# Attention A of a hybrid block on one core: output sums kept in PSUM over runs of head pairs, the norms inside the slots, sine products from PSUM

## The chip, the cores and the metric

The kernel runs on one core of a Trainium2 chip. The metric is the device time of one execution in microseconds (us). The times below are of three executions, and one more execution was profiled: all durations come from that one.

## The reference, cut to what matters

The program is a chain of four residual blocks over `x` of shape (8, 256, 256): attention A, a layer of experts, attention B, the experts again, each on a layer norm of `x`. The change touches attention A alone:

```
x = x + attn_a(layernorm(x));  x = x + ffn(layernorm(x));  x = x + attn_b(layernorm(x));  x = x + ffn(layernorm(x))

attn_a(x):                                # 16 heads, 2048 tokens, width 256
  q = x @ q_a_w.T @ q_b_w.T               # per head 64 plain + 64 rotated
  ckv = x @ kv_a_w.T                      # 64 compressed + 64 shared rotated keys
  k_pass, v = split(ckv[:, :64] @ kv_b_w.T)
  q_rot, k_rot = rope(q_rot), rope(k_rot) # (x0 cos - x1 sin, x1 cos + x0 sin)
  p = softmax([q_pass, q_rot] @ [k_pass, k_rot].T)   # 256 keys for each of 8 sequences
  return (p @ v, heads joined) @ o_w.T
```

## The kernel before, in words

Attention A is `attention_a` (from line 515). The 2048 tokens are four groups of 512 (`NG` = 4, `G` = 512), each of two sequences; the 16 heads are eight pairs (`HP` = 8). The work is 32 **slots**: slot n takes head pair n // 4 over token group n % 4, so one pair of heads goes over all four groups before the next begins. A slot has four **pairs** j = 0 to 3 (two sequences times two heads), and a pair is one 128x512 bank of scores.

Products that must be exact to fp32 are made of three fp32r matmuls (`matmul3`, lines 120 to 122) on upper and lower parts that ACT (upper, a cast) and DVE or POOL (lower, a subtraction) split.

The order of the work is written out by hand: each engine has a `step(n, j)` that lists what it does in that step, and all engines run the steps in the same order, tied by semaphores alone. In step (n, j):

- PE: the scores of the pair that lies six ahead (`LEAD` = 6) into bank `S(j)`, of which there are two; at j = 0 and 1 the query projection of slot n+3 for head h = j (`project_a`, five matmuls of 512 columns, lines 502 to 506) into `PROJ(h)`; at j = 2 the mix of probabilities and values of slot n (`mix`, line 668); the output product of a slot in two halves (`output`), the first at j = 3 of slot n+1, the second at j = 0 of slot n+2. The scores of pair g wait for the exponentials of pair g-2, which read the same bank.
- DVE: the row maxima of that pair (`row_max`, L846), the 32x32 transposes of the probabilities of the pair before it (`turn_squares`, L853), at j = 0 the product of the mixed values with the inverse sums (`normalise`, L869), at j = 0 and 1 the cosine product of the projection (`rope`, L481 through `times_table`), at j = 2 one sine product (`sines`), at j = 1 and 2 the addition of half an output bank to `x` (`add_out`, L874), at j = 3 the inverse of the row sums (`invert`, L858 and L861).
- ACT: the exponentials (`exps`, L771, two per pair), the upper part of the mixed values (`mixed_hi`), at j = 0 and 1 the swap of the two halves of the rotated rows out of PSUM (`swap_a`, L469 and L470, two copies of 32x512), at j = 2 and 3 the upper parts of the queries (`queries_hi`, L761).
- POOL: the lower part of the mixed values (L976), for head 0 the sine product (L481), for both heads the sum of cosine and sine products (`rotate`, L963), the lower parts of the queries (L971).
- SP, the queue that issues all DMAs: four DMAs that move the turned squares of each half slot (`move_squares`, L586), four that store the inverse sums (`store_inverse`, L592), two that load them spread over the partitions (`load_inverse`, L599), and once per head pair the weights (`load`, L579).

A rotated query is thus made so: PE projects, DVE multiplies all 128 rows with the cosines into `raw`, ACT copies rows 96 to 127 and 64 to 95 of the same PSUM bank, swapped, into `swapped`, POOL or DVE multiplies these with the sines in place, POOL adds.

The weights of a head pair are **folded** before use: matmuls on the staged weights (`fold_product`, L428, and `fold_output_product`, L511), upper parts on ACT (L440, L749), lower parts on DVE (L825, L830) and POOL (L982). The fold of the query weights of pair it lies in slot 4(it-2)+3, that of the output weights in the second slot of pair it-1; both keep two sets, taken in turn (`it % 2`).

Each half of an output product is closed in its slot (`start=True, stop=True`) and added to `x` two slots later: 64 additions of 128x512. In the last slots the layer norm of the next block begins: `norm_stats` (lines 59 to 67), `norm_rstd` on POOL (L73), `norm_rows` (L81), transposes on PE (L92), `norm_hi` (L100) and `norm_lo` (L108), groups 0 to 2 within or behind slots 30 and 31, all eight transposes of a group in a row into the two `PROJ` banks; group 3 is finished by the experts' block, whose first products (L1632) start at its opening.

## Time and profile before

| | |
|---|---|
| device time, median of 3 runs | 1533.96 us (1531.46 to 1535.32) |
| device time of the profiled execution | 1535.29 us |
| span of the profiled execution | 1533.5 us |
| mean granted clock of TensorE | 0.987 |
| PE busy | 1463.5 us, 95% |
| DVE busy | 1171.0 us, 76% |
| ACT busy | 835.8 us, 55% |
| POOL busy | 612.6 us, 40% |
| attention A's slots, first to last `aa_mixed` | 79.8 to 386.2 us |

How to read it: the device time is the span and about 1.8 us around it. A busy PE is not PE at its peak, since the ends of matmuls are modelled and overlap with the next one; how fast a stretch of matmuls goes is read from their starts. The busy shares are means over four blocks with different limits, and the change concerns only the stretch from about 54 us (the opening's end) to about 397 us (the first product of the experts).

### The profile page before, as it was taken

The numbers are of one execution on the slowest core, as the hardware profiler recorded it, in microseconds if no ns is written. First come the engines' busy times: TensorE is split into PE (matmuls) and PEld (weight loads), VectorE is DVE, ScalarE is ACT, GpSimd is POOL, SyncE is SP. The second block draws the span as 40 slices with busy tenths as digits, with TensorE's granted clock in tenths as the row PEclk, the third lists the DMA queues.
The fourth block names the chain that finished last, engine by engine and source line by source line (L and its number), as shares of the span: only waits on it lengthen the run. The fifth ranks groups of instructions, "written<-read, shape, count | busy, mean of one in ns | idle before, by whom it ended". The sixth has DMA issues, their size and how long they took to land. (4 is left out here: it accounts for less than half of the span.)

```text
span 1533.5 us, 26670 instructions
## 1 busy us (share of the span) xinstructions
PE 1463.5 (95%) x8904; PEld 1262.6 (82%) x8904; DVE 1171.0 (76%) x2661; ACT 835.8 (55%) x2040; POOL 612.6 (40%) x484
## 2 busy tenths in 40 slices
PE   8899999998799999988999999999999879999998
PEld 6677777776688888877899999989999868888887
DVE  7889999999765555587888888888888777555554
ACT  4788888885432333326766666666666433333322
POOL 2577777875100000017766666666666210000000
PEclk9899999999999999998999999999999999999999
DMA  2265555555210000003222222213222200010001
GB/s 101 53 161 142 154 145 151 148 129 149 82 41 22 22 21 0 1 1 91 62 70 61 71 63 64 75 42 80 73 50 49 56 22 21 21 42 21 0 0 56
DMA packets 73155, 100.16 MB, mean 65 GB/s; under 512 B 10304, under 2 KB 63552, under 8 KB 73024
## 3 DMA queue, kind: packets, MB, share of 16 engines
q1 hardware_dynamic: 73024, 98.55, 24.3%
q8 instruction: 66, 1.08, 0.3%
q14 instruction: 65, 0.53, 0.1%
HBM read 37.56 MB, written 2.23 MB: 26 GB/s over the span
## 5 line engine op out<-in xcount | busy, mean ns | idle before, releaser
L1834 DVE TENSOR_TENSOR f_hidden<-ps,f_silu 128x512 f32<-128x512 f32 x128 | 87.6, 689 | 201.7 <-PE ps L122 201.6
L481 POOL TENSOR_TENSOR ab_swapped<-ab_swapped,const 128x512 f32<-128x512 f32 x126 | 162.9, 1293 | 167.6 <-ACT ab_swapped L476 167.6
L1725 ACT ACTIVATE f_silu<-ps 128x512 f32<-128x512 f32 x128 | 76.3, 598 | 276.8 <-PE ps L122 276.8
L120 PE MATMUL ps<-xh,f_wl 128*128 128x512 f32 x512 | 203.2, 397 | 1.6 <-DVE f_hidden L1834 1.6
L121 PE MATMUL ps<-xl,f_wh 128*128 128x512 f32 x512 | 202.8, 396 | 0.0
L122 PE MATMUL ps<-xh,f_wh 128*128 128x512 f32 x512 | 202.5, 396 | 0.0
L1536 POOL TENSOR_TENSOR ab_qk<-ab_qk,ab_swapped 128x512 f32<-128x512 f32 x126 | 172.5, 1369 | 9.9
L1304 ACT ACTIVATE ab_probs<-ab_probs,ab_negmax 128x128 f32<-128x128 f32 (+1 forms) x256 | 114.6, 448 | 82.6 <-DVE ab_negmax L1407 80.6
L73 POOL TENSOR_TENSOR rstd<-shifted,minus_half 128x4 f32<-128x4 f32 x16 | 16.2, 1013 | 339.6 <-DVE shifted L67 339.6
L771 ACT ACTIVATE aa_probs<-ps,aa_negmax 128x256 f32<-128x256 f32 x256 | 119.2, 471 | 47.1 <-DVE aa_negmax L846 44.0
L120 PE MATMUL ps<-f_wh,f_hl 128*128 128x256 f32 x512 | 144.2, 282 | 0.4 <-DVE x L1850 0.4
L121 PE MATMUL ps<-f_wl,f_hh 128*128 128x256 f32 x512 | 143.9, 281 | 0.0
L122 PE MATMUL ps<-f_wh,f_hh 128*128 128x256 f32 x512 | 143.8, 281 | 0.0
L1431 DVE SCALAR_TENSOR_TENSOR x<-ps,ab_inv,x 128x256 f32<-128x256 f32 x256 | 118.8, 465 | 7.8 <-PE ps L122 3.1
L1733 ACT CAST f_hh<-f_hidden 128x512 fp32r<-128x512 f32 x128 | 78.8, 617 | 77.4 <-DVE f_hidden L1834 77.4
L481 DVE TENSOR_TENSOR ab_qk<-ps,const 128x512 f32<-128x512 f32 x128 | 87.2, 687 | 41.2 <-PE ps L122 40.8
L122 PEld LDWEIGHTS ps<-xh,f_wh 128*128 128x128 f32 x512 | 96.3, 188 | 23.4
L120 PEld LDWEIGHTS ps<-xh,f_wl 128*128 128x128 f32 x512 | 96.4, 188 | 23.1 <-DVE f_hidden L1834 2.4
L121 PEld LDWEIGHTS ps<-xl,f_wh 128*128 128x128 f32 x512 | 96.4, 188 | 20.4
L120 PE MATMUL ps<-xh,b_wl 128*128 128x512 f32 x256 | 105.9, 414 | 4.3 <-ACT ab_swapped L476 3.5
L1417 DVE STREAM_TRANSPOSE ab_squares<-ab_probs 128x384 f32<-128x384 f32 x128 | 109.7, 858 | 0.0
L1850 DVE SCALAR_TENSOR_TENSOR x<-ps,f_col,x 128x256 f32<-128x256 f32 x256 | 107.5, 476 | 1.6 <-PE ps L122 1.5
(210 smaller groups left out, 4377.5 us busy)
## 6 DMA issues: line engine op xcount, KB each, us to landing
ab_probsT<-ab_squares SPq DMA_DIRECT2D x128, 192.0 KB, 3.6
aa_probsT<-f_stages SPq DMA_DIRECT2D x128, 128.0 KB, 2.6
b_stages<-keys SPq DMA_DIRECT2D x128, 128.0 KB, 2.7
f_stages<-wf_in SPq DMA_DIRECT2D x16, 768.0 KB, 4.5
aa_spread<-aa_inv_line SPq DMA_DIRECT2D x64, 128.0 KB, 3.0
b_stages<-wb_qkv_in SPq DMA_DIRECT2D x8, 768.0 KB, 6.3
a_stage<-wa_in SPq DMA_DIRECT2D x8, 608.0 KB, 4.3
x<-x_in SPq DMA_DIRECT2D x4, 512.0 KB, 7.0
```

Of the source, the lines that this page charges most:

```text
L120: nc.tensor.matmul(out, ll, rh, start=start, stop=False)
L121: nc.tensor.matmul(out, lh, rl, start=False, stop=False)
L122: return nc.tensor.matmul(out, lh, rh, start=False, stop=stop)
L481: return engine.tensor_tensor(by_batch(out), by_batch(src), table(c, rows, col), ALU.mult)
L771: ins = nc.scalar.activation(probs[:, j, q, :], S(j)[:, q * T:(q + 1) * T], ACT.Exp, bias=negmax[:, j, q:q + 1], accum_out=total[:, s % 2, ...
L1304: ins = nc.scalar.activation(probs[:, j, span[q]], probs[:, j, span[q]], ACT.Exp, scale=-1.0, bias=negmax[:, j, q:q + 1], accum_out=total[ ...
L1417: nc.vector.transpose(out=squares[:, s % 2, :, :, j, :], in_=probs[:, j].rearrange("p (k i b) -> p b k i", k=3, b=4)).then_inc(squares_don ...
L1431: nc.vector.scalar_tensor_tensor(out=c.x[:, at, :], in0=bank[:, h * D:(h + 1) * D], scalar=inv[:, s, 2 * h + t // 2, t % 2:t % 2 + 1], in1 ...
L1536: nc.gpsimd.tensor_tensor(rows, rows, other, ALU.add).then_inc(rotated, 1)
L1733: nc.scalar.copy(hh[:, s % 2, m, :], hidden[:, m, :]).then_inc(hi_done, 1)
L1834: nc.vector.tensor_tensor(hidden[:, m, :], UP(m), silu[:, m, :], ALU.mult).then_inc(hid_done, 1)
L1850: ins = nc.vector.scalar_tensor_tensor(out=c.x[:, at, :], in0=OUT(i)[:, t, :], scalar=col[:, e, at:at + 1], in1=c.x[:, at, :], op0=ALU.mul ...
```

## The change

1. **Order of the slots.** `RUN_HEADS = [(0,), (1, 2, 3), (4, 5, 6, 7)]`: run 0 is pair 0 over the four groups (slots 0 to 3), run 1 takes for each group the pairs 1, 2, 3 in turn (slots 4 to 15), run 2 the pairs 4 to 7 (slots 16 to 31).
2. **Output in PSUM.** Within a run the output products of one group add up in the same bank: `start` only where a slot opens a run for its group, `stop` and `add_out` only where it closes one. 24 additions are left of 64.
3. **Folds.** Query and output weights are folded together in one piece (`fold`): PE at j = 3 of slots 0, 1, 5, 10, 12, 14, ACT and DVE at j = 0 of the next slot, POOL's part in the next slot too; the loads are issued by SP at the end of slots 0, 1, 2, 6, 11, 13 (its own order), each behind a wait for POOL's part of the fold before. Four sets of query weights and a set of output weights for each pair live partly in corners of `xh` and `xl` that nothing else needs then.
4. **Sines.** DVE multiplies rows 64 to 127 of the PSUM bank with the sines straight behind the cosine product, into rows 0 to 63 of `swapped`; only then is `rope_read` raised, for which ACT's swap waits. The swap copies rows 32 to 63 and 0 to 31 of `swapped` (SBUF) to rows 64 to 127; POOL's sum is now a difference. POOL's and DVE's sine products on `swapped` go.
5. **Norms in the slots.** Group g of the next block's norm for g = 0, 1, 2 goes to slots 21, 25, 29 and the two behind each: statistics at j = 2, `norm_rstd` at the end of POOL's slot, rows at j = 0 of the next, four transposes into the bank `FOLDED` at j = 2 and four at j = 0 of the slot after, each split on ACT and DVE at j = 3 and j = 1.
6. **The end.** The last slot's output goes into the same `OUT` banks; 12 filling matmuls stand before and 12 behind it.

The diff, cut to its core:

```diff
+    RUN_HEADS = [(0,), (1, 2, 3), (4, 5, 6, 7)]
+        RUNS = [(it, s) for its in RUN_HEADS for s in range(NG) for it in its]
+        RUN_OF = [run * NG + s for run in range(len(RUN_HEADS)) for s in range(NG) for _ in RUN_HEADS[run]]
+        opens = lambda n: n == 0 or RUN_OF[n] != RUN_OF[n - 1]
+        closes = lambda n: n == SLOTS - 1 or RUN_OF[n] != RUN_OF[n + 1]
+        FOLD_SLOT = {2: 0, 3: 1, 4: 5, 5: 10, 6: 12, 7: 14}
+        LOAD_SLOT = {2: 0, 3: 1, 4: 2, 5: 6, 6: 11, 7: 13}
+        FINISH = {4 * g + 2 * HP + 5: g for g in range(NG - 1)}
...
         def _(sp):
-                if s == 2 and it + 2 < HP:
-                    load(it + 2)
+                if n in loads:
+                    load(loads[n])
...
         def _(pe):
+            def fold(it):
+                pe.wait_ge(stage_in, 16 * (it + 1))
+                pe.wait_ge(wo_lo, it)
+                fold_product(nc, FOLD(it)[:, 0:P], stage, 0).then_inc(fold_ready, 1)
+                pe.wait_ge(fold_ready, it)
+                fold_product(nc, FOLD(it)[:, P:2 * P], stage, 1)
+                fold_output_product(nc, FOLD(it)[:, 2 * P:], stage).then_inc(wo_ready, 1)
...
             def output(n, i):
+                if opens(n):
+                    after(pe, out_added, 2 * RUN_OF[n] + i - 1)
-                    ins = matmul3(nc, bank[:, t * D:(t + 1) * D], ..., True, True)
+                    ins = matmul3(nc, OUT(i)[:, t * D:(t + 1) * D], ..., opens(n) and t == 0, closes(n) and t == 1)
...
             def step(n, j):
+                if j == 3 and n in folds:
+                    fold(folds[n])
                 if j == 2:
                     mix(n, 0)
                     mix(n, 1)
+                if j == 2 and finish(n - 1) is not None:
+                    turn_rows(finish(n - 1), 0)
+                if j == 0 and finish(n - 2) is not None:
+                    turn_rows(finish(n - 2), 1)
...
         def _(act):
             def swap(n, h):
                 act.wait_ge(rope_read, 2 * n + h + 1)
                 after(act, rotated, 0 if n == 1 else 2 * n + h - 1)
-                swap_a(nc, first_bank(n, h), swapped_of(n, h)).then_inc(swap_done, 1)
+                turned = swapped_of(n, h)
+                nc.scalar.copy(turned[64:96], turned[32:64])
+                nc.scalar.copy(turned[96:128], turned[0:32]).then_inc(swap_done, 1)
...
         def _(dve):
             def rope(n, h):
-                times_table(nc.vector, c, raw_of(n, h), first_bank(n, h), ALL_ROWS, C_COSA).then_inc(rope_read, 1)
+                times_table(nc.vector, c, raw_of(n, h), first_bank(n, h), ALL_ROWS, C_COSA)
+                after(dve, swap_done, 0 if n == 1 else h + 1 if n == 2 else m - 1)
+                times_table(nc.vector, c, swapped_of(n, h)[0:64], first_bank(n, h)[64:128], ROT_ROWS, C_SINA).then_inc(rope_read, 1)
...
             def step(n, j):
+                if j == 0 and n - 1 in folds:
+                    fold(folds[n - 1])
-                if j == 2 and n + 3 < SLOTS:
-                    sines(n + 3, 1)
-                if j in (1, 2) and n >= 2:
+                if j in (1, 2) and n >= 2 and closes(n - 2):
                     add_out(n - 2, j - 1)
+                if j == 2 and finish(n) is not None:
+                    normalise_stats(finish(n))
+                if j == 0 and finish(n - 1) is not None:
+                    norm_rows(nc, c, norm, dve, finish(n - 1))
+                if j == 3 and finish(n - 1) is not None:
+                    norm_lower(finish(n - 1), 0)
+                if j == 1 and finish(n - 2) is not None:
+                    norm_lower(finish(n - 2), 1)
...
         def _(pool):
             def rotate(n, h):
-                if n < 3:
-                    pool.wait_ge(sin_done, 2 * n + h + 1)
-                elif h == 1:
-                    pool.wait_ge(sin_done, n + 4)
-                else:
-                    pool.wait_ge(swap_done, 2 * n + h + 1)
-                    times_table(nc.gpsimd, c, other, other, ROT_ROWS, C_SINA).then_inc(side_done, 1)
-                    pool.wait_ge(side_done, n - 2)
+                pool.wait_ge(swap_done, 2 * n + h + 1)
                 pool.wait_ge(rope_read, 2 * n + h + 1)
-                nc.gpsimd.tensor_tensor(rows, rows, other, ALU.add).then_inc(rotated, 1)
+                nc.gpsimd.tensor_tensor(rows, rows, other, ALU.subtract).then_inc(rotated, 1)
...
+                if n - 1 in folds:
+                    fold_rest_parts(folds[n - 1])
```

## Rows read from the trace of the kernel before

**Rows 1.** Waits in 40 to 400 us: us in total, times, longest.

```profile
ACT aa_probs L771 <- DVE aa_negmax L846: 44.0, 36, 1.8
...
PEld ps L120 <- ACT aa_probs L771: 24.1, 45, 0.9
...
DVE a_wl L825 <- ACT a_wh L440: 8.3, 6, 1.4
...
DVE a_wol L830 <- ACT a_woh L749: 7.1, 7, 1.5
```

**Rows 2.** DVE's timeline over one slot: start us, us, engine, line.

```profile
190.31 0.65 DVE L846 TENSOR_REDUCE aa_negmax<-ps 128x2 f32<-128x512 f32 x1
...
191.50 0.65 DVE L869 TENSOR_TENSOR aa_mixed<-ps,aa_spread 128x512 f32<-128x512 f32 x1
192.08 0.67 DVE L481 TENSOR_TENSOR a_raw<-ps,const 128x512 f32<-128x512 f32 x1
192.68 0.67 DVE L846 TENSOR_REDUCE aa_negmax<-ps 128x2 f32<-128x512 f32 x1
...
193.89 0.65 DVE L481 TENSOR_TENSOR a_raw<-ps,const 128x512 f32<-128x512 f32 x1
...
195.66 0.69 DVE L853 STREAM_TRANSPOSE keys<-aa_probs 128x512 f32<-128x512 f32 x1
196.38 1.44 DVE L481 TENSOR_TENSOR a_swapped<-a_swapped,const 64x512 f32<-64x512 f32 x1
197.85 0.69 DVE L874 TENSOR_TENSOR x<-ps,x 128x512 f32<-128x512 f32 x1
198.46 0.68 DVE L846 TENSOR_REDUCE aa_negmax<-ps 128x2 f32<-128x512 f32 x1
...
201.27 0.65 DVE L869 TENSOR_TENSOR aa_mixed<-ps,aa_spread 128x512 f32<-128x512 f32 x1
```

**Rows 3.** Groups by line and form, whole span: busy us, mean ns, idle before.

```profile
L469 ACT COPY a_swapped<-ps 32x512 f32<-32x512 f32 x62 | 35.8, 578 | 1.6 <-DVE a_raw L481 0.2
...
L481 DVE TENSOR_TENSOR a_swapped<-a_swapped,const 64x512 f32<-64x512 f32 x33 | 31.4, 952 | 1.5 <-ACT a_swapped L470 0.5
```

**Rows 4.** Timelines of ACT, PE, DVE at the hand-overs of scores.

```profile
175.92 0.47 ACT L771 ACTIVATE aa_probs<-ps,aa_negmax 128x256 f32<-128x256 f32 x1
...
176.99 0.39 PE L120 MATMUL ps<-kh,a_ql 128*128 128x256 f32 x1 [0.51 <-ACT aa_probs L771]
...
364.89 0.39 PE L120 MATMUL ps<-kh,a_ql 128*128 128x256 f32 x1
...
365.89 0.69 DVE L846 TENSOR_REDUCE aa_negmax<-ps 128x2 f32<-128x512 f32 x1 [0.19 <-PE ps L122]
```

**Rows 5.** PE's timeline over slots with and without a fold.

```profile
177.80 0.40 PE L502 MATMUL ps<-q1h,a_wl 128*128 128x512 f32 x1
...
181.65 1.37 PE L428 MATMUL ps<-a_stage 64*128 64x64 f32 x8
...
187.98 0.40 PE L502 MATMUL ps<-q1h,a_wl 128*128 128x512 f32 x1
...
202.32 0.65 PE L511 MATMUL ps<-a_stage 128*64 128x256 f32 x4
```

**Rows 6.** DVE's timeline: mixed values of slots 0 and 29.

```profile
79.82 0.69 DVE L869 TENSOR_TENSOR aa_mixed<-ps,aa_spread 128x512 f32<-128x512 f32 x1 [0.24 <-DMA aa_spread<-aa_inv_line]
...
369.06 0.69 DVE L869 TENSOR_TENSOR aa_mixed<-ps,aa_spread 128x512 f32<-128x512 f32 x1 [0.26 <-issue]
```

**Rows 7.** The page's DMA issues: KB each, us to landing.

```profile
aa_spread<-aa_inv_line SPq DMA_DIRECT2D x64, 128.0 KB, 3.0
```

**Rows 8.** Timeline of the end of attention A: SP, DVE, PE.

```profile
379.63 1.13 SPq L599 DMA_DIRECT2D aa_spread<-aa_inv_line  x2
...
393.34 1.40 DVE L62 BATCH_NORM_STATS2 moments<-x 128x6 f32<-128x256 f32 x4
...
396.88 0.47 PE L1632 MATMUL ps<-xl,wr 128*128 128x512 f32 x1 [2.28 <-PEq L525]
```

More of the change, by code:

```diff
@@ L250, in fold @@
                 for h in range(2):
[L251 removed]
+                    ins = fold_upper(nc, SPARE[:, h * P:(h + 1) * P], stage, a.wh[0], h)
                 ins.then_inc(fold_hi, 1)
[L253 removed]
+                nc.scalar.copy(a.woh[0], SPARE[:, 2 * P:]).then_inc(a.wo_hi, 1)
             def first_swap(h):
@@ L669, in mix, with output @@
                 ins.then_inc(pv_done, 1)
-            def output(n, i, bank=None):
-                (it, s), half = at(n), n // NG % 2
+            def output(n, i):
+                it, s = at(n)
                 if i == 0:
@@ L679, in output, with turn_rows @@
                         pe.wait_ge(wo_lo, it + 1)
-                if bank is None:
-                    bank = OUT(i)
-                    after(pe, out_added, 2 * n + i - 1)
-                else:
-                    pe.wait_ge(exp_done, PAIRS * SLOTS)
+                if opens(n):
+                    after(pe, out_added, 2 * RUN_OF[n] + i - 1)
                 for t in range(2):
                     tok = slice((2 * i + t) * P, (2 * i + t + 1) * P)
-                    ins = matmul3(nc, bank[:, t * D:(t + 1) * D], (mh[:, s % 2, tok], ml[:, s % 2, tok]), (woh[:, half, :], wol[:, half, :]), True, True)
+                    ins = matmul3(nc, OUT(i)[:, t * D:(t + 1) * D], (mh[:, n % 2, tok], ml[:, n % 2, tok]), (woh[it], wol[it]), opens(n) and t == 0, closes(n) and t == 1)
                 ins.then_inc(out_ready, 1)
+            def turn_rows(g, k):
+                if k == 0:
+                    pe.wait_ge(norm.normed_done, g + 1)
+                after(pe, norm.lo_done, KD * g + k)
+                if g == 0:
+                    pe.wait_ge(wo_lo, HP)
+                for i in range(TG):
+                    ins = nc.tensor.transpose(FOLDED[:, i * P:(i + 1) * P], norm.normed[:, i, k * P:(k + 1) * P], c.ident)
+                ins.then_inc(norm.turned, 1)
             def step(n, j):
-                it, s = at(n)
                 if exists(n, j, LEAD):
@@ L721, in _ @@
             for j in range(2, PAIRS):
-                scores(0, 0, j)
-            fold_query(1, 0)
+                scores(0, j)
+            fold(1)
             for j in range(LEAD - PAIRS):
-                scores(0, 1, j)
+                scores(1, j)
             for n in range(SLOTS):
@@ L792, in step @@
                     queries_hi(n + 3, j - 2)
-                if n == SLOTS - 1 and j == 0:
-                    norm_hi(nc, c, norm, act, 0, norm_banks)
             swap(1, 0)
             swap(1, 1)
-            exps(0, 0, 0)
+            exps(0, 0)
             queries_hi(1, 0)
-            exps(0, 0, 1)
+            exps(0, 1)
             swap(2, 0)
             queries_hi(1, 1)
-            exps(0, 0, 2)
+            exps(0, 2)
             swap(2, 1)
-            exps(0, 0, 3)
-            fold_query(1)
-            exps(0, 1, 0)
+            exps(0, 3)
+            fold(1)
+            exps(1, 0)
             queries_hi(2, 0)
-            exps(0, 1, 1)
+            exps(1, 1)
             queries_hi(2, 1)
@@ L814, in _, with fold @@
             mixed_hi(SLOTS - 1)
-            for s in range(1, NG - 1):
-                norm_hi(nc, c, norm, act, s, norm_banks)
         @block.vector
         def _(dve):
-            def fold_query(it):
+            def fold(it):
                 dve.wait_ge(fold_hi, it)
+                dve.wait_ge(wo_hi, it + 1)
                 for h in range(2):
-                    (upper, source), _ = fold_parts(FOLD(it)[:, h * P:(h + 1) * P], stage, wh[:, it % 2], h)
-                    ins = nc.vector.tensor_tensor(wl[:, it % 2, :, h, 0:KVR], source, upper.bitcast(F32), ALU.subtract)
+                    (upper, source), _ = fold_parts(FOLD(it)[:, h * P:(h + 1) * P], stage, wh[it % 4], h)
+                    ins = nc.vector.tensor_tensor(wl[it % 4][:, :, h, 0:KVR], source, upper.bitcast(F32), ALU.subtract)
                 ins.then_inc(fold_lo, 1)
-            def fold_output(it, bank):
-                dve.wait_ge(wo_hi, it + 1)
-                nc.vector.tensor_tensor(wol[:, it % 2, :], bank[:, 0:D], woh[:, it % 2, :].bitcast(F32), ALU.subtract).then_inc(wo_lo, 1)
+                nc.vector.tensor_tensor(wol[it], FOLD(it)[:, 2 * P:], woh[it].bitcast(F32), ALU.subtract).then_inc(wo_lo, 1)
             def rope(n, h):
@@ L1000, in _ @@
                         queries_lo(n + 3, h)
-                if n + 2 >= SLOTS:
-                    norm_rstd(nc, c, norm, pool, n + 2 - SLOTS)
-                    pool.wait_ge(norm.rstd_done, n + 3 - SLOTS)
-                if fold_after(n):
-                    fold_rest_parts(fold_after(n))
+                if finish(n) is not None:
+                    norm_rstd(nc, c, norm, pool, finish(n))
+                    pool.wait_ge(norm.rstd_done, finish(n) + 1)
             mixed_lo(SLOTS - 1)
-            for s in range(2, NG):
-                norm_rstd(nc, c, norm, pool, s)
+            norm_rstd(nc, c, norm, pool, NG - 1)
 PARTS_B = [slice(0, 2), slice(2, 3)]
```

201 lines of the change are left out of this document (81 added, 120 removed).

## The prediction

> **What bounds the kernel now.** I read the waits of attention A first, then DVE's timeline over one slot, then the timelines of ACT and PE beside it, last the end of the stage. In the waits the exponentials wait for the row maxima 36 times, and PE's score loads for the exponentials 45 times, while DVE waits for little but the folds, 8.3 + 7.1 us [rows 1]. In its timeline DVE runs without a hole from one product of mixed values (191.50) to the next (201.27): this slot is DVE's work, 9.77 us [rows 2]. From mixed values 0 to 29 it is 369.06 - 79.82 = 289.2 us for 29 slots, 9.97 each, folds included [rows 6]. So DVE bounds the slots. PE is close: from a projection at 177.80 to the same one a slot later at 187.98 it does not wait, 10.18 us, of which the fold's products take 181.65 to about 182.95 and a gap of 0.1 ahead, 1.40 [rows 5]. A slot of PE alone is 8.8 us. Behind the slots comes a tail: mixed values 29 at 369.06, statistics of group 3 at 393.34, the experts' first product at 396.88 [rows 6, 8].
>
> **DVE's work in a plain slot.** The slot of 9.77 us has one sine product on SBUF: from the transpose before it (195.66) to the addition behind it (197.85) is 2.19 us, where a transpose alone advances 0.61 (maxima and transpose 1.21, from 192.68 to 193.89, the maxima 0.60), so it costs 1.58 [rows 2]. An addition advances 0.61 (197.85 to 198.46), two are 1.2 [rows 2]. Without both: 9.77 - 1.58 - 1.2 = 7.0. Added are two sine products from PSUM. No row shows one. The nearest is the cosine product, also PSUM times table, 0.65 to 0.67 us [rows 2]. In its present place it advances only 0.60 (192.08 to 192.68) [rows 2], since the next instruction starts before it ends; but behind the transpose of 0.69 the sine product, which starts at row 64 instead of 0, starts 0.72 later, after the end [rows 2]. I take this for the new ones as well: cosine 0.70, sine 0.70, so each sine adds 0.80. By the overlap it would add 0.60 (lower end); by the mean of the old sine products, 0.95 long [rows 3], it adds 1.08 (upper end). 7.0 + 1.6 = **8.6 us**, and 9.8 in a slot in which two additions are left.
>
> The Trainium skill ("VectorE: DVE Perf Modes", section "Two Vector instructions with no wait between them") has this as a rule: an instruction whose input or output starts in another group of 32 partitions than the last one's is held until all earlier ones are done. It speaks against the change, and by it the sum is the same as mine; without it each plain slot would be 0.3 us shorter.
>
> The long sine products beside it are 1.44 us here and 0.95 in the mean against 0.67 for the cosine one of twice the rows [rows 2, 3]; both their inputs lie in SBUF, and POOL works at the same time. [...]
>
> **A new chain.** ACT's swap now waits for both products, and on ACT the exponentials of step j = 2 stand behind the swap of step j = 1. PE's first scores of the next slot reuse the bank they read. The way round, from row maxima to row maxima: maxima to mixed values 191.50 - 190.31 = 1.19; mixed values 0.58; cosine and sine of head 0, 1.40; maxima and transpose of j = 1, 193.89 - 192.68 = 1.21; cosine and sine of head 1, 1.37 [rows 2]: together 5.75. Hand-over 0.1 and two swap copies 2 x 0.59 [rows 3], 1.3. Exponentials to the start of the scores 176.99 - 175.92 = 1.07; scores to the start of their maxima 365.89 - 364.89 = 1.00 [rows 4]. Sum **9.1 us** (the same chain now is 7.6, far under 9.77). So a plain slot will be 9.1 us, not 8.6: neither DVE nor PE but the chain through DVE, ACT and PE binds.
>
> **The 29 slots.** Base: 28 x 9.14 = 255.9, and slot 29, which has no projection but two additions and statistics, 9.1. Then what rises above the chain:
> - Additions. Slots 2, 3, 4, 8, 11, 17, 21, 25 hold two of them (those in 5 and 14 hide behind a fold's slot): 9.8 - 9.14 = 0.65 each, 5.2.
> - Folds, five in these slots (1, 5, 10, 12, 14). PE: 1.40 and the output part's 0.65, less one change of operands, 1.95; 8.8 + 1.95 - 9.14 = 1.6 [rows 5]. In the next slot DVE has three subtractions behind the first maxima, on the chain, 0.25 + 0.25 + 0.36 = 0.86. ACT's five casts end before DVE needs them: the 15.4 us of fold waits [rows 1] go, but they only become PE's time. 5 x 2.5 = 12.3.
> - Norms of groups 0 and 1 (slots 21 to 23, 25 to 27): statistics 2.0 (the four rows of 1.40 and the aggregation behind, to 395.27 [rows 8]), rows 1.35 on the chain, two subtractions of 0.6 of which 0.05 and 0.05 to 0.3 show, PE's transposes hidden at j = 2 and 0.2 at j = 0: 3.7 each, 7.3.
> - SP. Five loads (slots 1, 2, 6, 11, 13) wait for POOL's part of the fold just made, 5.9 us into the slot, and behind each stand the moves of the next squares (2.6) and the load of the inverse sums (1.2 to issue, 3.0 to land [rows 7]). It lands 12.1 us in, where DVE wants it at 11.2 to 11.9: 0.3 to 0.9 each, 3.5 in all. The third weights land later than PE's fold wants them, 1.2. Together 4.7; lower end 0.
>
> Sum 255.9 + 9.1 + 5.2 + 12.3 + 7.3 + 4.7 = 294.5. The same way of adding, for the kernel before, is 29 x 9.4 (7.0, additions 1.2, the mean sine product 1.2), 6.0 of fold subtractions and 15.4 of waits, less 2.4 in slot 29: 291.6, where 289.2 was measured. So I take 2.4 off: 292.1, **2.9 more** than before.
>
> **Slot 0 and what is ahead.** Before, slot 0 took 8.1 us (no output, no mixed values). Now PE has a fold there and waits some 0.7 us for its weights: 10.0. With half a us in the prologue, where the first fold is now whole, **+2.4**. The cosine and sine products there cost what the four sine products on SBUF did.
>
> **The tail.** From mixed values 29: norm rows of group 2 (1.4) delay the last maxima, the last transpose ends 4.5 later; SP moves the squares until 7.1 and stores the inverse sums until 8.7; they are loaded from 10.0 (before: one such load issued at 379.63 [rows 8]), land at 13.6, and only then can the mixed values 31 be made. Upper and lower part 2.1, output 1.4, additions 1.3 with the first one overlapping: statistics of group 3 at 18.1, ended at 20.1, POOL's root at 21.3, the experts' first product at 21.4. Before, the first and the last of these stood at 24.3 and 27.8 [rows 6, 8], since the norms of three groups, each with a step on POOL, lay between: **-6.4**. POOL loses 29 products, which lie on no path: cost nothing, gain nothing.
>
> **Sum:** 2.9 + 2.4 - 6.4 = -1.1 us against the profiled 1535.29; its span is 1533.5. The median of the runs is 1533.96, so I forecast **1533 us**. About 0.3%, 4.6 us, is what a measurement can tell from no change.
>
> **The rivals.**
> - *The relief shows (faster).* The sine products overlap as cosine ones do, each adds 0.60: the chain is 8.84, the additions' slots 9.4, and SP's waits don't reach DVE. 28 x -0.3 and -4.7: 1520 us. For it: cosine products do overlap [rows 2], SP has several us of slack now. Against it: the one row with another start row does not overlap [rows 2]. Chance 0.30. [...]
> - *The sine product is dear (slower).* On DVE, behind the cosine one, it takes 0.95 us as the old ones did in the mean [rows 3]. Two of them lie on the chain: 28 x 0.56 = 15.7, 1549 us. It decides from 0.10 us more than my 0.67 (28 x 0.2 = 5.6). Against it: the cosine product with the same kinds of operands is 0.67 at most. Chance 0.12.
> - *SP holds the squares.* The five loads delay moves and inverse sums by 2 us more than I count: +9, 1542. For it: SP is one queue in order. Against it: DVE hardly waits for `aa_spread` now. Chance 0.13.
> - *It does not do what it says:* PE's output matmuls are as many as before, so keeping sums in PSUM saves PE nothing; that is in my sum.
>
> **How the numbers follow.** My forecast has 0.45, with its own range 1526 to 1541. Faster by over 0.3% (under 1529.4): nearly all of the first rival and 0.07 of the forecast's, 0.36. Slower (over 1538.6): the two other rivals and 0.04 of the forecast, 0.28. Within: 0.36. The range for 8 in 10 reaches into the faster rival and into the third, 1517 to 1546.
>
> **What would show it.** DVE's timeline: cosine and sine at 0.70 each, not 0.60. Mean distance of mixed values in slots 7 to 9, 16 to 20: 9.1; 8.8 speaks for the first rival, over 9.5 for the second. ACT's waits for the maxima turn into waits for the sine product, and PE still waits for exponentials. The additions fall to 24; the slots of folds are the longest, near 10.8, beside slots 21 and 25. Mixed values that wait for the DMA of `aa_spread` in slots 2, 3, 7, 12, 14 speak for SP. The experts' first product should start 21.4 us behind mixed values 29. I am wrong if plain slots stay under 8.9 or above 9.4.

## Result: 1554.76 us, slower by 1.2%

The changed kernel takes 1554.76 us (median of 4 runs, 1550.88 to 1555.86) beside 1534.64 us for the kernel before on the same chip: a ratio of 1.0124, 95% interval 1.0104 to 1.0143. The forecast of 1533 us and its range, 1517 to 1546, were both missed on the slow side.

The page of the changed kernel, its first lines:

```profile
span 1552.9 us, 26585 instructions
...
PE 1468.5 (95%) x8928; PEld 1271.8 (82%) x8928; DVE 1172.4 (75%) x2650; ACT 836.6 (54%) x2040; POOL 574.8 (37%) x455
```

The span grew by 19.4 us, yet PE, DVE and ACT are busy for at most 5 us more, PE's weight loads beside them for 9, and POOL for 38 less. The time lies in waits and holds. DVE's timeline of the changed kernel has the two ends of the 29 slots, as [rows 6], and PE's timeline the start of the experts, as [rows 8]:

```profile
83.92 0.65 DVE L863 TENSOR_TENSOR aa_mixed<-ps,aa_spread 128x512 f32<-128x512 f32 x1
...
390.61 0.65 DVE L863 TENSOR_TENSOR aa_mixed<-ps,aa_spread 128x512 f32<-128x512 f32 x1
...
413.60 0.47 PE L1606 MATMUL ps<-xl,wr 128*128 128x512 f32 x1 [1.61 <-PEq L527]
```

The first mixed values come 4.1 us later (forecast 2.4). The 29 slots take 390.61 - 83.92 = 306.7 us, 17.5 more than the 289.2 before (forecast 2.9). From there to the experts' first product it is 22.99 us, 4.8 less than before (forecast 6.4 less). These make 16.8; the remaining 2.6 us lie behind the experts' start, where nothing was changed. That unchanged stretch takes 1136.6 us in the profile of the kernel before, 1139.3 in that of the changed kernel, and between 1134.7 and 1138.8 in the runs below, without a pattern that I can see. So of two kernels that differ by a few us, up to 4 can come from there.

The waits of the changed kernel in 40 to 430 us, as [rows 1] (us in total, times, longest):

```profile
ACT a_swapped L753 <- DVE a_swapped L481: 33.3, 56, 0.9
PE ps L120 <- ACT aa_probs L770: 28.6, 39, 1.7
...
ACT aa_probs L770 <- DVE aa_negmax L841: 22.6, 21, 3.0
...
DVE aa_mixed L863 <- issue: 8.1, 5, 2.9
...
DVE aa_mixed L863 <- DMA aa_spread<-aa_inv_line: 3.7, 1, 3.7
...
PE ps L428 <- DMA a_stage<-wa_in: 3.3, 2, 1.9
```

As foreseen, ACT's wait for the maxima (44.0 before) turned into one for the sine product, PE still waits for exponentials, and the waits of the fold on ACT are gone. New are DVE's waits for the spread inverse sums, and PE's for staged weights.

By form, in the same stretch (busy us, mean ns, idle before), as [rows 3]:

```profile
L481 DVE TENSOR_TENSOR a_swapped<-ps,const 64x512 f32<-64x512 f32 x60 | 41.6, 693 | 0.8
...
L753 ACT COPY a_swapped<-a_swapped 32x512 f32<-32x512 f32 x60 | 37.0, 617 | 33.4 <-DVE a_swapped L481 33.3
...
L868 DVE TENSOR_TENSOR x<-ps,x 128x512 f32<-128x512 f32 x24 | 16.1, 672 | 3.4 <-PE ps L122 3.1
...
L81 DVE TENSOR_SCALAR normed<-x,meanvar,rstd 128x256 f32<-128x256 f32 x16 | 10.6, 724 | 1.6 <-PEq L527 1.6
```

The sine product takes 693 ns, not 0.95 us: the "dear" rival is out. The additions are 24, as the change says. The last row is the surprise: the 16 normalised rows took 408 ns each in the kernel before and take 724 in the mean here. The row of the kernel before, in 40 to 430 us:

```profile
L81 DVE TENSOR_SCALAR normed<-x,meanvar,rstd 128x256 f32<-128x256 f32 x16 | 5.5, 408 | 2.4 <-POOL rstd L73 2.0 <-PEq L525 0.4
```

**One plain slot.** DVE's timeline of the changed kernel over a slot without fold, addition or norm (to be laid beside [rows 2]):

```profile
265.68 0.65 DVE L863 TENSOR_TENSOR aa_mixed<-ps,aa_spread 128x512 f32<-128x512 f32 x1
266.26 0.67 DVE L481 TENSOR_TENSOR a_raw<-ps,const 128x512 f32<-128x512 f32 x1
266.95 0.69 DVE L481 TENSOR_TENSOR a_swapped<-ps,const 64x512 f32<-64x512 f32 x1
267.67 0.69 DVE L841 TENSOR_REDUCE aa_negmax<-ps 128x2 f32<-128x512 f32 x1
...
268.39 0.71 DVE L847 STREAM_TRANSPOSE keys<-aa_probs 128x512 f32<-128x512 f32 x1
269.03 0.65 DVE L481 TENSOR_TENSOR a_raw<-ps,const 128x512 f32<-128x512 f32 x1
...
269.69 0.69 DVE L481 TENSOR_TENSOR a_swapped<-ps,const 64x512 f32<-64x512 f32 x1
...
270.42 0.69 DVE L841 TENSOR_REDUCE aa_negmax<-ps 128x2 f32<-128x512 f32 x1
...
272.74 0.71 DVE L847 STREAM_TRANSPOSE f_stages<-aa_probs 128x512 f32<-128x512 f32 x1 [0.31 <-ACT aa_probs L770]
...
273.78 0.69 DVE L841 TENSOR_REDUCE aa_negmax<-ps 128x2 f32<-128x512 f32 x1
274.39 0.70 DVE L847 STREAM_TRANSPOSE f_stages<-aa_probs 128x512 f32<-128x512 f32 x1
...
275.02 0.65 DVE L863 TENSOR_TENSOR aa_mixed<-ps,aa_spread 128x512 f32<-128x512 f32 x1
```

The slot is 9.34 us long. Starts are 0.69, 0.72 and 0.72 us apart from the cosine product over the sine product and the maxima to the transpose of step 0. Without a sine product it was 0.60 from cosine product to maxima and 1.21 for maxima and transpose together [rows 2]. So one sine product adds 2.77 - 1.81 = 0.96 us to the stretch from a cosine product to the next thing behind the transpose (266.26 to 269.03, against 192.08 to 193.89), not 0.80.

The other half of the chain is in the timelines of ACT and PE of the changed kernel, as [rows 4]:

```profile
270.42 0.62 ACT L753 COPY a_swapped<-a_swapped 32x512 f32<-32x512 f32 x1 [0.46 <-DVE a_swapped L481]
...
271.69 0.47 ACT L770 ACTIVATE aa_probs<-ps,aa_negmax 128x256 f32<-128x256 f32 x1
...
272.76 0.39 PE L120 MATMUL ps<-kh,a_ql 128*128 128x256 f32 x1 [0.99 <-ACT aa_probs L770]
```

Added up as the prediction did: maxima to mixed values 1.24 (273.78 to 275.02), mixed values 0.58, cosine and sine 1.41, maxima and transpose 1.36, cosine and sine 1.39, swap 1.27 (to 271.69), exponentials to scores 1.07, scores to their maxima 1.02 (to 273.78). The sum is 9.34, the measured slot. It has to be, since each term ends where the next one begins; it proves nothing about what binds. What speaks for the chain is that there is hardly any slack on it: ACT's swap waits 0.46 us for the sine product, and PE waits 0.99 for the exponentials behind the swap. At the last hand-over DVE does not wait for the scores; it comes to their maxima at the same moment by another way, behind a transpose that waited 0.31 for the same exponentials (272.74). DVE has no other hole in this slot.

**The slots by kind.** The periods are the differences of the starts of `aa_mixed` on DVE:

| slots | forecast | measured |
|---|---|---|
| plain (7, 9, 15, 16, 18 to 20, 24, 28) | 9.1 | 9.32 to 9.37 |
| two additions (3, 4, 8, 17) | 9.8 | 9.95 to 9.99 |
| folds (10, 12; 5, 14 with additions) | 11.6 | 11.44, 11.48; 11.85, 11.89 |
| fold in slot 1, late weights | 12.8 | 12.58 |
| with a load that holds SP (2, 6, 11, 13) | 0.3 to 0.9 over their kind | 1.29, 2.93, 0.64, 1.91 over |
| norms (21, 22; 25, 26) | 3.7 a group over their kind | 12.0, 13.2; 12.0, 13.2: 6.0 a group over |

28 x 9.33 + 9.02 (slot 29) + 5.0 (additions) + 12.6 (folds, the waits for weights among them) + 6.8 (late loads) + 12.0 (norms) is 306.7 again, since the parts are made of the periods themselves.

### The profile page after: what moved, and what is told of

It reads as the page before. It is cut to its first block and busy times, and to the rows that moved or that the text cites. A ratio compares the mean times of both kernels' runs of the same rounds, so it can differ in the third digit from the quotient of the medians.

```text
span 1552.9 us, 26585 instructions
## 1 busy us (share of the span) xinstructions
PE 1468.5 (95%) x8928; PEld 1271.8 (82%) x8928; DVE 1172.4 (75%) x2650; ACT 836.6 (54%) x2040; POOL 574.8 (37%) x455
## 5 line engine op out<-in xcount | busy, mean ns | idle before, releaser
L120 PE MATMUL ps<-kh,a_ql 128*128 128x256 f32 x256 | 80.8, 316 | 29.8 <-ACT aa_probs L770 28.6
```

Of the source, the lines that this page charges most:

```text
L120: nc.tensor.matmul(out, ll, rh, start=start, stop=False)
```

## The experiments

Every kernel is compared with the kernel before on the same chip, by the ratio; the changed kernel's is 1.0124. Each ratio is known to about 0.0015 to 0.002 either way, so a difference of two ratios, given below in us, to some 4 us. Slot times come from the profile; plain slots of one kernel agree there within a few hundredths of a us. In the diffs "..." stands for lines left out.

**The swap behind the exponentials.** In the changed kernel, both swaps one step later:

```diff
-                if j < 2 and n + 3 < SLOTS:
-                    swap(n + 3, j)
+                if 1 <= j < 3 and n + 3 < SLOTS:
+                    swap(n + 3, j - 1)
```

> The changed kernel with one order on ACT turned: the swap of head h for slot n+3 stands behind the exponentials of step h+1 instead of behind those of step h. Theory 1, the way round from row maxima through both sine products, the swap, the exponentials and the next scores binds (9.33 us in a plain slot): with the swap behind the exponentials it is gone, plain slots fall to 8.8 to 9.0 us (DVE's or PE's own work), slots with two additions stay at 9.95, about 7 to 9 us less than the changed kernel in all, near 1546 us. Theory 2, DVE's own work with its longer sine products binds: nothing moves, 1555 us within 2. Against both: POOL gets its rows later and the scores wait for the lower parts of the queries, slower than 1557 us.

Measured: 1568.69 us, ratio 1.0214 (1.0197 to 1.0231); plain slots 10.10 (slots 7 and 15 are 10.0). The theory missed; the sign is that of the third possibility named. The waits of this kernel in 40 to 430 us:

```profile
ACT aa_probs L770 <- DVE aa_negmax L841: 77.7, 66, 3.9
POOL a_raw L938 <- ACT a_swapped L754: 65.9, 30, 4.3
```

I took the query casts for the cause, which stand in ACT's list close behind the late swap and need POOL's rotation; the next run tests that. The trace of this kernel says otherwise. In a plain slot the exponentials of step 2 wait 0.45 us for their maxima (from 291.59), the second swap follows (292.63), then a query cast that waits for nothing (293.91), the exponentials of step 3 (294.44), and DVE's transpose waits for these:

```profile
295.49 0.71 DVE L847 STREAM_TRANSPOSE keys<-aa_probs 128x512 f32<-128x512 f32 x1 [1.02 <-ACT aa_probs L770]
```

Behind it come the mixed values (296.12, 10.10 after the last ones), both sine products and the maxima of step 2 again. The swap was not taken off the way round; it stands before the exponentials of step 3 instead of those of step 2.

**Swap and casts late.** The same, and head 0's query cast in step 3, head 1's in step 0 of the next slot:

```diff
-                if j >= 2 and n + 3 < SLOTS:
-                    queries_hi(n + 3, j - 2)
+                if j == 3 and n + 3 < SLOTS:
+                    queries_hi(n + 3, 0)
+                if j == 0 and n >= 1 and n + 2 < SLOTS:
+                    queries_hi(n + 2, 1)
```

> The kernel as changed with ScalarE's swap copies behind the exponentials (steps 1 and 2 of the slot instead of 0 and 1) and, unlike the run with the late swap, the query casts one step later too (head 0's in step 3, head 1's in step 0 of the next slot), so that ScalarE doesn't stand before a cast that waits for POOL's rotation. What it decides: whether the copies' place on the way to the exponentials is worth its 1.3 us per slot once nothing else is pushed back. Theory (the plain slot of 9.33 is the chain maxima, exponentials, copies, scores; POOL's order was the only thing that made the late swap lose): plain slots at PE's 8.8 to 9.0, some 8 to 12 us less in all, 1543 to 1547. Rival (the second head's query parts now reach PE too late, or POOL's subtraction for head 1 is late whatever ScalarE does): plain slots at 9.33 or above, 1555 or slower, with the waits on ScalarE's cast or on POOL's low part.

Measured: 1584.84 us, ratio 1.0335 (1.0317 to 1.0352); plain slots 10.30 (slots 7 and 15 are 9.5). The rival was right. Among the waits of this kernel is a new one, of DVE's cosine product for the buffer that POOL's low part still reads:

```profile
POOL a_ql L948 <- ACT a_qh L760: 68.1, 61, 6.5
...
DVE a_raw L481 <- POOL a_ql L948: 11.8, 18, 0.7
```

In a plain slot head 0's cast stands behind the second swap and the exponentials of step 3 (302.95), POOL's low part waits 0.27 for it (303.70), and the next cosine product waits 0.73 for the low part (305.11, 10.30 after the last one). So each of these two orders puts the swap on another closed way, and neither gives its place back. Whether the 1.27 us of the swap would be saved with nothing else pushed back, no run shows.

**Sine products over all 128 rows.** For slots up to 20, DVE multiplies the whole bank with the sine table (whose rows 0 to 63 are there as well) into a tile that the norm uses only later; ACT swaps rows 64 to 127 of that. Twice the rows, nothing left out, and every operand starts at row 0:

```diff
...
-                times_table(nc.vector, c, swapped_of(n, h)[0:64], first_bank(n, h)[64:128], ROT_ROWS, C_SINA)
+                times_table(nc.vector, c, sined[:, h, :], first_bank(n, h), ALL_ROWS, C_SINA)
```

> The changed kernel, but for slots up to 20 the sine product is taken over all 128 rows into the free buffer of the norm rows, from which ACT swaps, so that its operands start in row 0 as those of its neighbours do. Theory 1, an instruction that starts in another group of partitions holds itself and the next ones: cosine 0.69, sine 0.72 and the maxima behind 0.72 each become 0.60, a slot's chain is 0.4 us and DVE's work 0.66 us shorter up to slot 17, plain slots there at 8.9 us, about 6 us less in all, 1549 us. Rival, the distances are due to PSUM or to the table operand and not to the start row: nothing moves, 1555 us, and starts stay 0.72 apart.

Measured: 1546.06 us, ratio 1.0066 (1.0049 to 1.0082), about 9 us less than the changed kernel's. In the profiles the 29 slots take 5.0 us less; of the rest, 3.8 lie behind the experts' start, where nothing differs. The timelines of DVE and PE in this kernel:

```profile
135.99 0.65 DVE L869 TENSOR_TENSOR aa_mixed<-ps,aa_spread 128x512 f32<-128x512 f32 x1
136.57 0.67 DVE L481 TENSOR_TENSOR a_raw<-ps,const 128x512 f32<-128x512 f32 x1
137.16 0.68 DVE L481 TENSOR_TENSOR normed<-ps,const 128x512 f32<-128x512 f32 x1
137.76 0.68 DVE L847 TENSOR_REDUCE aa_negmax<-ps 128x2 f32<-128x512 f32 x1
138.36 0.69 DVE L853 STREAM_TRANSPOSE keys<-aa_probs 128x512 f32<-128x512 f32 x1
138.97 0.66 DVE L481 TENSOR_TENSOR a_raw<-ps,const 128x512 f32<-128x512 f32 x1
...
140.15 0.68 DVE L847 TENSOR_REDUCE aa_negmax<-ps 128x2 f32<-128x512 f32 x1
...
142.60 0.39 PE L120 MATMUL ps<-kh,a_ql 128*128 128x256 f32 x1 [0.67 <-ACT aa_probs L773]
```

From cosine product to cosine product it is 2.40 us, against 2.77 in the changed kernel, although each sine product now does twice the rows. Plain slots are 8.86 to 8.89 (7, 9, 15, 16), and 9.33 again from slot 18 on, whose sine products belong to slot 21 and later, which were left narrow. The chain's terms on DVE are 0.58 us shorter here (135.99 to 140.15, against 265.68 to 270.42), while the slot fell by 0.46. At 8.87 it is next to the 8.8 us that PE alone was put at, but PE still waits 0.67 us here for the exponentials behind the swap: the chain seems to bind still.

**Sines as before, the rest as changed.** PE, ACT and POOL wait as in the kernel before, the swap reads PSUM, one sine product per slot is DVE's in SBUF and one POOL's:

```diff
...
-                after(dve, swap_done, 0 if n == 1 else h + 1 if n == 2 else m - 1)
-                times_table(nc.vector, c, swapped_of(n, h)[0:64], first_bank(n, h)[64:128], ROT_ROWS, C_SINA).then_inc(rope_read, 1)
+            def sines(n, h):
+                dve.wait_ge(swap_done, 2 * n + h + 1)
+                rows = swapped_of(n, h)[64:128]
+                times_table(nc.vector, c, rows, rows, ROT_ROWS, C_SINA).then_inc(sin_done, 1)
```

> The changed kernel with the sine products as they were before: swap out of PSUM first, head 0's sine product on POOL, head 1's on DVE in SBUF, sum on POOL. Theory 1, the sine products from PSUM make the chain and lengthen DVE's work: plain slots fall from 9.33 to PE's 8.8 or 8.9 us, slots with two additions from 9.95 to 9.4, some fold work hides, 13 to 18 us less than the changed kernel, 1537 to 1542 us. Rival, the loss sits in the new order of slots, folds and loads: no more than 5 us less, above 1549 us.

Measured: 1544.42 us, ratio 1.006 (1.0043 to 1.0077), a little above the band; plain slots mostly 8.98 to 9.02 (slot 15 is 8.86, slot 16 9.50), with additions 9.45 to 9.50.

**The sine part alone, in the kernel before.** The opposite edit in the other kernel:

```diff
...
-                times_table(nc.vector, c, raw_of(n, h), first_bank(n, h), ALL_ROWS, C_COSA).then_inc(rope_read, 1)
+                times_table(nc.vector, c, raw_of(n, h), first_bank(n, h), ALL_ROWS, C_COSA)
+                after(dve, swap_done, 0 if n == 1 else h + 1 if n == 2 else m - 1)
+                times_table(nc.vector, c, swapped_of(n, h)[0:64], first_bank(n, h)[64:128], ROT_ROWS, C_SINA).then_inc(rope_read, 1)
```

> The kernel before with the sine part of the change alone: both sine products on DVE straight from PSUM behind the cosine product, swap on ACT behind them, difference on POOL; slots, folds, additions and norms as before. Theory 1, each such sine product adds 0.93 us to DVE (itself, and its neighbours held): DVE's slot of about 9.4 us loses one sine product of 1.2 and gets two of 0.93, 10.1 us where no fold is near, 15 to 20 us slower than the kernel before, 1552 us. Rival, what costs is the new order of slots and not the sine products: within 4 us of the kernel before.

Measured: 1547.36 us, ratio 1.0068 (1.0053 to 1.0083); slots without a fold 9.95, with one 10.76 and 11.28. That is 10 us more than the kernel before beside the 15 to 20 expected, and well over the rival's 4. The sine part costs 0.7% by itself and, by the run above, 0.6% within the change (1.0124 against 1.006).

**All loads late.** The weights' load behind the load of the inverse sums, in SP's next slot:

```diff
                     load_inverse(n - 1)
+                if n - 1 in loads:
+                    load(loads[n - 1])
                 move_squares(n, 1)
                 store_inverse(n)
-                if n in loads:
-                    load(loads[n])
```

> The changed kernel with each load of weights moved on SP's queue from the end of its slot to behind the load of the inverse sums in the next, so that nothing it waits for stands ahead of the moves of squares and inverse sums. Theory 1, SP is held by the loads and DVE then waits for the inverse sums (6.4 us in slots 2, 6, 11, 13): these waits go, 5 to 6 us less, 1549 us. Rival, these waits lie beside work of PE: nothing moves, or PE waits as long for the weights of folds 2 and 3, 1555 us within 2.

Measured: 1555.51 us, ratio 1.012 (1.0103 to 1.0136). The rival was right: slots 6, 11 and 13 fell to 9.34, 9.95 and 9.34, but the weights of the first two folds came too late, mixed values 0 at 91.2 and slot 1 15.16 us long. The waits of this kernel:

```profile
PE ps L428 <- DMA a_stage<-wa_in: 9.9, 2, 7.0
```

**Loads mixed.** The first three loads where the change has them, the last three behind the inverse sums (`if n - 1 in loads and n > 3`, and `if n in loads and n < 3` in the old place).

> The changed kernel with the loads of weights 5, 6 and 7 moved behind the load of the inverse sums in SP's next slot, and the loads of weights 2, 3 and 4 where the change put them. Theory 1, SP held by its loads costs DVE its waits for the inverse sums in slots 6, 11 and 13 (2.9, 0.6 and 1.9 us), and the early loads are wanted early: 5 us less than the changed kernel, 1549 us, with these slots at 9.34, 9.95 and 9.34. Rival, the waits come back elsewhere: 1554 us.

Measured: 1547.65 us, ratio 1.0066 (1.005 to 1.0082), about 9 us less. Slots 6, 11 and 13 are 9.34, 9.95 and 9.33: 0.64 to 2.92 us each, 5.5 together, as the theory has it. But slot 23 grew from 9.39 to 10.76, and the 29 slots together take 4.0 us less in the profile. The tail is 1.2 longer, and 4.0 more are gained behind the experts' start, where nothing differs; that part is not explained.

**Norms at the end, as before.** `FINISH` is emptied, and statistics, rows, transposes and splits of groups 0 to 2 stand in and behind slots 30 and 31 again, in the `PROJ` banks, and the filling matmuls of the end are 6 and 6 instead of 12 and 12:

```diff
-        finish = lambda n: FINISH.get(n)
+        finish = lambda n: None
+        norm_banks = [PROJ(0), PROJ(1)]
...
             output(SLOTS - 2, 1)
+            norm_turn(nc, c, norm, pe, 1, norm_banks)
```

> The changed kernel with the norms of groups 0 to 2 taken out of the slots and put where the kernel before has them, in and behind the last two slots. Theory 1, the norms in the slots cost more than they give: slots 21 to 23 and 25 to 27 take 12 us more than plain ones, most of it DVE's norm rows, 3.4 us long beside POOL instead of 1.4; without them 12 us less there and 4 to 6 us more at the end, 6 to 8 us less in all, 1547 us. Rival, the tail grows by as much as the slots lose: 1555 us within 2.

Measured: 1542.42 us, ratio 1.0037 (1.0021 to 1.0053), 13 us less, where 6 to 8 were expected: the 29 slots take 13.2 less in the profile, the tail only 2.6 more. Slots 21, 22, 25 and 26 are 9.95, 9.33, 9.95 and 9.34. The normalised rows are short again in this place, as the groups by form of this kernel in 40 to 430 us show:

```profile
L81 DVE TENSOR_SCALAR normed<-x,meanvar,rstd 128x256 f32<-128x256 f32 x16 | 5.5, 408 | 2.4 <-POOL rstd L73 2.0 <-PEq L527 0.4
```

**The rows alone.** The changed kernel with the normalised rows of groups 0 to 2 left out (one element each in their place, behind the same waits), and with them their part of the output:

```diff
-                    norm_rows(nc, c, norm, dve, finish(n - 1))
...
+                    nc.vector.tensor_scalar(norm.normed[:, 0, 0:1], c.x[:, g * TG, 0:1], norm.meanvar[:, g % 2, 0, 0:1], norm.rstd[:, g % 2, 0:1], ALU.subtract, ALU.mult).then_inc(norm.normed_done, 1)
```

> The kernel as changed without the four rows that VectorE normalises for each of token groups 0 to 2 (12 instructions; a single one-element instruction with the same waits stands for each group, so the waits for POOL's inverse deviation stay). Their part of the output is left out. What it decides: what those rows cost beside POOL's work. Theory (they cost what their row shows, 3.44 us for four, all of it on VectorE's path): slots 22 and 26 fall from 13.23 to 10.0 to 10.4 us, slot 30 by some 1.5 to 2.3, together 7.5 to 8.5 us: 1547 beside 1554.8. Rival (the group is late for the reason that POOL's inverse deviation is late and the turns wait for PE, and the rows are worth their 0.35 us each, 1.4 us per group): slots 22 and 26 stay at 11.8 or above, 1550 to 1552.

Measured: 1546.38 us, ratio 1.0074 (1.0057 to 1.0091), about 8 us less. Slots 22 and 26 are 10.08 us, 3.15 less. The theory was right. The timeline of the changed kernel shows why four rows cost so much there, DVE and POOL over slot 22:

```profile
307.68 3.44 DVE L81 TENSOR_SCALAR normed<-x,meanvar,rstd 128x256 f32<-128x256 f32 x4
...
307.72 1.27 POOL L951 TENSOR_TENSOR aa_ml<-aa_mixed,aa_mh 128x512 fp32r<-128x512 f32 x1
...
309.07 1.26 POOL L938 TENSOR_TENSOR a_raw<-a_raw,a_swapped 64x512 f32<-64x512 f32 x1
...
311.15 0.69 DVE L841 TENSOR_REDUCE aa_negmax<-ps 128x2 f32<-128x512 f32 x1
```

Two POOL products lie within the 3.44 us. Where POOL is idle, four rows take 1.38 to 1.41 us. The longest single row here took 1.46 us, the shortest 0.40.

**All three together.** Wide sine products in all slots, norms at the end, loads mixed. Nothing of the computation is left out.

> The changed kernel with three parts mended together: the sine product over all 128 rows in all slots, the norms at the end as before, loads 5 to 7 behind the inverse sums. Theory 1, the three losses are separate and add up (9 us measured for the slots up to 17 and 5 us more for the others, 7 us, 5 us): 26 us less than the changed kernel, 1526 to 1531 us, faster than the kernel before by 5 to 9 us, plain slots 8.9, slots with two additions 9.35. Rival, another limit (PE's own 8.8 us and its folds) takes over and they add up to less: 1533 us or more, no better than the kernel before.

Measured: 1524.05 us (5 runs, 1522.02 to 1526.51), ratio 0.9914 (0.99 to 0.9928): faster than both kernels. It takes 13 us less than the kernel before, where 5 to 9 were expected. The three savings were 0.0058, 0.0087 and 0.0058 of the time; taken off 1.0124 they give 0.9921. That this agrees is partly luck: the wide products now run in the slots behind 17 as well, some 5 us more, and two of the three savings had some 4 us from the stretch where nothing differs. In the slots alone the three gave 5.0 + 13.2 + 4.0 us, and all together 30.7. The page of this kernel:

```profile
span 1524.7 us, 26535 instructions
...
PE 1458.5 (96%) x8904; PEld 1266.0 (83%) x8904; DVE 1151.8 (76%) x2650; ACT 837.5 (55%) x2040; POOL 575.9 (38%) x455
```

Its plain slots are 8.86 us long, those with additions 9.35; the first mixed values still stand 3.7 us later than before, and the fold of slot 1 still makes that slot 12.5.

## Why the prediction was wrong

- **What bounds the slots: right as far as the trace shows.** The waits on the forecast's chain through DVE, ACT's swap and PE are there, and the plain slots are 9.33, put at 9.1. The run that was to prove it by moving the swap did not, since the swap stayed on a closed way; the full rows run bears it out, since terms on the chain that grew 0.58 shorter made the slot 0.46 shorter. The forecast's own terms add up to 9.12, and 9.14 was used; that is 0.6 us over 28 slots.
- **The sine products: the step that failed most.** The text said the sine product itself starts only when the cosine product has ended, and counted 0.80. It let the two instructions behind it go free. They are held too (0.72 and 0.72 us from start to start, instead of 0.60 and 0.61), and each sine product adds 0.96. DVE's own work in a plain slot is thus 7.0 + 2 x 0.96 = 8.9 us instead of 8.6, and on the chain lies the first of the two held pairs (maxima and transpose 1.36, not 1.21), with smaller differences 0.2 us per slot, 5.3 us in all. (On the chain the sine product itself had its right size, 1.41 against 1.40; what was put at nothing is what it does to the two instructions behind it.) The sign of the sine part alone is shown both ways, 1.0068 in the kernel before and 1.0124 against 1.006 in the changed one. With all operands at row 0, in the full rows run, the hold is gone although the work is doubled. That run changed the number of rows together with the start row. What tells the two apart is the transpose: it and the maxima just ahead of it both cover 128 rows from row 0, and it is held nonetheless. The Trainium skill ("VectorE: DVE Perf Modes", section "Two Vector instructions with no wait between them") compares each input's group of 32 partitions with that of the last instruction that read the same memory. The sine product reads PSUM and the table from row 64, so by that rule the maxima (PSUM from row 0) and the transpose (SBUF from row 0) are held as well, and the trace agrees with all three. The prediction gave the rule without the part on the memory, applied it to one instruction, and said that the sum would be the same.
- **Norms in the slots: wrong by 4.7 us.** The rows were put at 1.35 us per group, from the end of the kernel before, where POOL is idle. Beside POOL they take 3.44, and two groups cost 12.0 instead of 7.3. POOL's work beside it was looked at for the sine products and not for the rows. That POOL is the cause is read from the overlap in the timeline and from the short rows where POOL is idle; no run took POOL's two products away. A step between is on record: the rows of group 2 (from 391.18) have a single POOL product beside them (392.05, 1.30 us) and take 2.32. So with none, one and two products beside them four rows take 1.38, 2.32 and 3.44 us. The Trainium skill ("SBUF — State Buffer", section "SBUF: two separate sides") has GpSimd and a VectorE instruction in a two-port mode exclude each other for a whole instruction, which fits a row of 1.46 us beside a POOL product of 1.27; in which mode the rows ran, no run here shows.
- **SP's queue: seen, but too small.** 3.5 us were put down for late inverse sums, 6.8 were measured, 2.93 of them in slot 6. SP's own instructions and DVE's mixed values over that slot, in the timeline of the changed kernel:

```profile
139.53 0.65 DVE L863 TENSOR_TENSOR aa_mixed<-ps,aa_spread 128x512 f32<-128x512 f32 x1
...
143.13 0.36 SPq L585 DMA_DIRECT2D a_stage<-wa_in  x1
...
143.61 2.54 SPq L592 DMA_DIRECT2D b_stages<-keys  x4
...
146.25 1.21 SPq L605 DMA_DIRECT2D aa_spread<-aa_inv_line  x2
...
151.79 0.69 DVE L863 TENSOR_TENSOR aa_mixed<-ps,aa_spread 128x512 f32<-128x512 f32 x1 [2.85 <-issue]
```

  The order is the one foretold: load, squares, inverse sums. But from the issue of the inverse sums to the mixed values it is 5.5 us, where 1.2 and 3.0 were put down; with the load issued behind them (the mixed run) this wait is gone. The slower of the two transfers of these sums took 4.8 us to land, and 3.6 in the mixed run; whether the weights on their way ahead of them slow them, no run tests. "SP holds the squares", a rival for +9, came to 3.3 of its 9. The mixed loads took 5.5 us off three slots and gave 1.4 back in slot 23.
- **The calibration: wrong by 2.4 us.** The same way of adding gave 2.4 too much for the kernel before, and I took it off. Carried over to the changed kernel, this was 2.4 too little: with the parts at their measured sizes the slots add up without it. I take it that the excess belonged to DVE's work in the kernel before and not to the chain here; that is not shown.
- **Folds and additions: right.** Folds 12.6 with their waits for weights, against 13.5; additions 5.0 against 5.2.
- **Slot 0 and the tail: right in sign, 1.7 and 1.6 us too good.** In slot 0 the wait for the second weights was 1.9 us and not 0.7; the other 0.5 was not looked for. In the tail the norm rows of group 2 took 2.32 us instead of 1.4, mixed values 31, which wait for the inverse sums, were made 14.25 us behind mixed values 29 instead of 13.6, and the experts began at 22.99 instead of 21.4.
- **Together.** In the 29 slots: 5.3 (chain, slot 29 among it) + 4.7 (norms) + 3.3 (SP) + 2.4 (calibration) - 0.2 (additions) - 0.9 (folds) = 14.6, the whole of what was missed there (306.7 - 292.1). 1.7 and 1.6 at the ends and 2.6 behind them make 20.5, which is the span's +19.4 against -1.1. Against 1533 the profiled 1554.8 is 21.8 more, since the profiled execution of the kernel before lay 1.3 above its median. The 2.6 behind the experts' start have no cause shown, nor have the 0.9 of the tail that come behind mixed values 31.

Why the change gives so little back is seen in the same terms. The 40 additions that it saves took 0.61 us each on DVE, 24 us, and the fold's waits were 15.4. But DVE's own work no longer binds, as far as the trace shows: a chain binds that runs through the sine products and the swap that waits for them; the folds' waits became PE's own time; and the norms that left the tail, with all else that changed there, gave 4.8 us in it and took 12.0 in the slots. In the changed kernel the old sine products make plain slots of 9.0 us, the narrow ones from PSUM 9.33, the wide ones 8.86.

## What to carry to other kernels

On VectorE, count a product on a part of the partitions by what it does to the instructions behind it, one for each memory that it reads at another start row (here 0.96 us for a product of 0.69); where the other rows hold nothing that hurts, work on all 128. Work moved out of an idle tail into a busy stretch is priced by a row beside the same neighbours, above all if it reads SBUF next to GpSimd. And on a queue in order, a transfer that waits belongs behind those that somebody needs soon, unless it is itself the first that is needed.

## What the runs showed that I had not expected

- A product of twice the rows made the slot shorter: 8.87 instead of 9.33 us.
- Normalised rows of 128x256 cost 3.44 us per four beside GpSimd, 1.4 without it, and 3.15 us of slot time.
- ACT's copy of 32x512 takes 617 ns from SBUF, 578 from PSUM [rows 3]; four copies a slot make this 0.16 us, half of it on the chain.
- Where a slot has a hole, TensorE's clock falls as well. The stretches of a fold's slot, a plain slot and a norm's slot of the changed kernel (length, busy us of PE, PEld, DVE, ACT, POOL, granted clock, DMA share, GB/s):

```profile
83.92:96.50 12.58, 11.10 (x70) 8.65 (x69) 9.57 (x19) 9.19 (x28) 7.11 (x6) 0.91 0.50 155
...
265.68:275.02 9.34, 8.35 (x60) 6.76 (x59) 8.77 (x17) 7.95 (x25) 6.22 (x6) 1.00 0.62 145
305.69:318.92 13.23, 10.05 (x62) 8.11 (x61) 12.66 (x21) 8.49 (x26) 7.25 (x7) 0.87 0.41 93
```

In the plain slot the clock stays at its upper level, 2.4 GHz (1.00), with PE busy for 8.35 of 9.34 us. In the norm's slot, where PE waits for the rows, the mean is 0.87.
